# One-hot matrices of the geometric stage: loaded and scaled on ScalarE, or compared and scaled on VectorE

## What is computed

```
# first graph layer (attention)
w = ex / denom[dst]
agg = segment_sum(w[:, :, None] * V[src], dst, num_segments=N)

# second graph layer (geometric)
act = softmax(full)                    # full = 64 scores and 192 zeros
msgs = act * tp2_flat
agg = segment_sum(msgs, dst, num_segments=N)
```

## Time and profile before

| | us |
|---|---|
| median of 3 runs (lowest, highest) | 3384.34 (3380.32, 3385.76) |
| the profiled execution | 3386.62 |
| its span, first to last instruction | 3384.7 |
| PE, DVE, ACT, POOL busy | 2547.7, 2239.3, 1415.8, 1500.8 |

### The profile page before, as it was taken

How to read it: one execution, slowest core, us unless ns; L and a number is a source line. 1 busy time by engine, 2 the same in 40 slices (tenths; PEclk the granted TensorE clock), 3 DMA queues, 4 the chain that set the end, 5 groups by cost and what they waited for, 6 DMA issues and landing times. The chain is left out here.

```text
span 3384.7 us, 46930 instructions
## 1 busy us (share of the span) xinstructions
PE 2547.7 (75%) x13339; PEld 1901.5 (56%) x13339; DVE 2239.3 (66%) x5226; ACT 1415.8 (42%) x5164; POOL 1500.8 (44%) x1409
## 2 busy tenths in 40 slices
PE   6555666634777777775369957999999969999997
PEld 3434454422444444443246845666666658789997
DVE  8655565525888888886866828999999962022221
ACT  1000000000555555556232237888888841233332
POOL 0566666615555545550100025666666503434442
PEclk9965656655788878887679978999999979999999
DMA  4223232276677767773200046666666652322223
GB/s 111 67 53 88 71 88 76 84 40 193 199 211 223 214 199 217 212 214 97 73 0 1 8 142 180 199 199 197 201 200 201 164 159 84 71 46 39 38 36 65
DMA packets 288291, 419.61 MB, mean 124 GB/s; under 512 B 118887, under 2 KB 200651, under 8 KB 287720
## 3 DMA queue, kind: packets, MB, share of 16 engines
q0 software_dynamic: 91456, 234.61, 24.5%
q1 hardware_dynamic: 167218, 180.43, 20.0%
q10 hardware_dynamic: 29366, 1.56, 0.8%
HBM read 358.58 MB, written 61.03 MB: 124 GB/s over the span
## 5 line engine op out<-in xcount | busy, mean ns | idle before, releaser
L1314 POOL DMA_INDIRECT g_rows<-h_d,src x416 | 452.8, 1088 | 550.5 <-POOLq L74 319.0
L966 POOL DMA_INDIRECT a_strip<-kv_d,src x416 | 402.1, 966 | 423.0 <-DVE x L1109 204.9
L326 POOL DMA_INDIRECT rec_d<-o_rec_in,o_place x392 | 398.0, 1015 | 293.6 <-DVE o_place L554 171.6
L997 ACT ACTIVATE x<-a_strip,x 128x64 f32<-128x64 f32 x1664 | 408.4, 334 | 220.5 <-PE a_psv L1042 165.9
L1042 PE MATMUL a_psv<-x 128*125 128x260 f32 x832 | 316.1, 488 | 170.5 <-issue 90.4
L410 PE MATMUL o_ps_base<-o_run,o_lo_hot_t 125*128 125x26 f32 x782 | 172.2, 374 | 211.5 <-issue 109.1
L1042 PEld LDWEIGHTS a_psv<-x 128*125 128x125 f32 x832 | 156.0, 223 | 258.6 <-issue 135.4
L410 PEld LDWEIGHTS o_ps_base<-o_run,o_lo_hot_t 125*128 125x128 f32 x782 | 160.2, 304 | 221.2 <-issue 114.4
L1412 PE MATMUL g_psa<-g_msg,g_hot 128*125 128x256 f32 x832 | 232.4, 403 | 56.6 <-issue 52.2
L1022 PE MATMUL a_psq<-q,a_ht 125*128 x1248 | 221.7, 339 | 21.5 <-DVE a_ht L1100 15.6
L1412 PEld LDWEIGHTS g_psa<-g_msg,g_hot 128*125 128x125 f32 x832 | 140.1, 188 | 172.8 <-issue 159.3
(11 more groups left out here) (436 smaller groups left out, 5441.5 us busy)
## 6 DMA issues: line engine op xcount, KB each, us to landing
a_row<-rows_d SPq DMA_DIRECT2D x104, 256.0 KB
hot_d<-x SPq DMA_DIRECT2D x104, 250.0 KB
g_hot<-hot_d SPq DMA_DIRECT2D x104, 250.0 KB
o_row<-dst_rows_d SPq DMA_DIRECT2D x98, 256.0 KB
o_row_lo<-lo_rows_d SPq DMA_DIRECT2D x98, 128.0 KB
e_w<-in_L_ffn_W1p SPq DMA_DIRECT2D x8, 1024.0 KB
e_w<-in_L_ffn_W2p SPq DMA_DIRECT2D x8, 1024.0 KB
a_strip<-kv_d,src POOLq DMA_INDIRECT x416
```

Of the source, the lines that this page charges most:

```text
L326: pool.indirect_dma_start(out=m.rec_d[:, :], out_offset=bass.IndirectOffsetOnAxis(ap=place[s % RP][:, u:u + 1], axis=0), in_=rec_in[:, U * ...
L966: pool.indirect_dma_start(out=strip[:, lane.start + u, place:place + 2, :].rearrange("p a d -> p (a d)"), out_offset=None, in_=m.kv_d[:, : ...
L997: act.activation(msg[b][:, u, h, 0:HD], strip[:, lane.start + u, place, h * HD:(h + 1) * HD], ACT.Copy, scale=w[:, k * U + u, h:h + 1])
L1314: pool.indirect_dma_start(out=rows[r][:, u, 64:576], out_offset=None, in_=m.h_d[:, :], in_offset=bass.IndirectOffsetOnAxis(ap=m.src[:, s * ...
```

## The change

The attention stage no longer stores `hot`, and the DRAM tensor `hot_d` is gone. The geometric stage no longer loads it. There DVE makes `hot` with four tensor_scalar instructions per step, one per group: the row of node numbers 0 to 124 is compared with the edge's number and multiplied by the reciprocal `rz`, both per-partition numbers. They stand behind the fourth addition and ahead of L1498. ACT's four L1363 are gone, and `s_xm` is raised by the last L1358. PE waits for the new semaphore too.

```diff
@@ attention
-        s_kept = [sem(f"a_kept{b}") for b in range(2)]
...
-        KEEP = LAG + R
...
-            for s in range(STEPS + KEEP):
-                if s < STEPS:
-                    if s >= R:
-                        sp.wait_ge(s_ht, s - R + 1)
-                    sp.dma_start(rowb[s % R][:, :], m.rows_d[s:s + 1, :].to_broadcast([128, 2 * W])
-                                 ).then_inc(s_row[s % R], 16)
-                v = s - KEEP
-                if v >= 0:
-                    sp.wait_ge(s_hot, v + 1)
-                    sp.dma_start(m.hot_d[v], hot[v % 2]).then_inc(s_kept[v % 2], 16)
-            for b in range(2):
-                sp.wait_ge(s_kept[b], 16 * len(range(b, STEPS, 2)))
+            for s in range(STEPS):
+                if s >= R:
+                    sp.wait_ge(s_ht, s - R + 1)
+                sp.dma_start(rowb[s % R][:, :], m.rows_d[s:s + 1, :].to_broadcast([128, 2 * W])
+                             ).then_inc(s_row[s % R], 16)
...
                 if s >= 2:
                     dve.wait_ge(s_mm, U * (s - 1))
-                    dve.wait_ge(s_kept[s % 2], 16 * (s // 2))
@@ geometric
-        s_hot = [sem(f"g_hot_{r}") for r in range(RH)]
+        s_hot = sem("g_hot")
...
-        @block.sync
-        def _(sp):
-            for s in range(STEPS):
-                if s >= RH:
-                    sp.wait_ge(s_prod, 2 * (s - RH) + 2)
-                sp.dma_start(hot[s % RH][:, :, :], m.hot_d[s]).then_inc(s_hot[s % RH], 16)
...
                 for u in range(U):
-                    act.activation(msg[s % RM][:, u, 64:256], vec[b][:, u, :], ACT.Copy, scale=en[s % 3][:, u:u + 1])
-                h = hot[s % RH]
-                act.wait_ge(s_hot[s % RH], 16 * (s // RH) + 16)
-                act.wait_ge(s_rz, 2 * s + 2)
-                for u in range(U):
-                    last = act.activation(h[:, u, :], h[:, u, :], ACT.Copy, scale=rz[b][:, u:u + 1])
+                    last = act.activation(msg[s % RM][:, u, 64:256], vec[b][:, u, :], ACT.Copy, scale=en[s % 3][:, u:u + 1])
                 last.then_inc(s_xm, 1)
...
                     pe.wait_ge(s_xm, s + 1)
+                    pe.wait_ge(s_hot, s + 1)
...
                 add(3)
+                if not last:
+                    if s >= RH:
+                        dve.wait_ge(s_prod, 2 * (s - RH) + 2)
+                    dve.wait_ge(s_rz, 2 * s + 2)
+                    for u in range(U):
+                        t = s * U + u
+                        done = dve.tensor_scalar(hot[s % RH][:, u, :], m.iota[:, 0:P], m.rec[:, t, R_LO:R_LO + 1],
+                                                 rz[b][:, u:u + 1], ALU.is_equal, ALU.mult)
+                    done.then_inc(s_hot, 1)
                 if not last:
                     dve.tensor_tensor(t1[:, :, :], t1[:, :, :], ps_o[b][:, :, 0:64], ALU.add).then_inc(s_t1, 1)
@@ build
-        m.hot_d = dram("hot_d", [STEPS, EP, U, P])
```

## The result

The changed kernel takes **3493.93 us**, the median of 4 runs (3491.08 to 3497.41); the kernel before, on the same chip, 3382.33 (3377.04 to 3385.76). The ratio is 1.0332, 95% interval [1.0313, 1.0351]: slower by 3.3%. The forecast was 3488 within 3436 to 3530.

A forecast was written before the change was run, and what follows sets the result against it. It took DVE's own instruction stream to bound the geometric stage. Added comparisons 110 us, less 5 for attention and 1 at the end, gave +104: 3488 us, measured from the median 3384.34, with a range of 3436 to 3530.

The forecast's parts named there:

- The main term: Geometric stage: four added DVE instructions paid in full, 0.27 us each, 1.08 a step over 102 steps, 110 us.
- The rivals by price: Geometric comparisons: 0.15 us each gives 3439 us, chance 0.10; 0.36 each, the whole duration, gives 3525 us, chance 0.12.
- The new waits cost nothing.: Geometric stage, DVE: waiting for `s_rz` and `s_prod` adds 0 us, the fourth addition covering the reciprocal.
- never waits: Geometric stage: DVE, busy 97% of the steady stretch, waits for no other engine in a step of 6.58 us.
- by the same 1.08 us: Geometric stage: DVE's stream after the comparisons, POOL's gathers and PE all move by 1.08 us a step.
- Attention: Attention stage: removing the stores of `hot` gains 5 us, with bounds of 0 and 95.5 us.
- attention pays it back: Rival: attention regains 95.5 us of DVE's idle time, leaving 3390 us, no measurable change; chance 0.05.
- The start: Start of the geometric stage: DVE idles 13.15 and 0.95 us in the first two steps, so 102 steps pay.
- The 1 us at the end: End of the geometric stage: DVE's wait of 1.31 us for PE before the last additions shrinks, gaining 1 us.
- TensorE's clock: Steady geometric stretch: PE's busy share falls from 92% to 79%, its granted clock staying at 1.00.
- The condition of the rival: Geometric stage: PE's clock falls, costing time below 0.79; at 0.75 it adds 45 us, giving 3533; chance 0.06.
- The other signs: Steady geometric stretch: period 7.6 to 7.7 us, DVE at 97% or more, ACT idling 1.3 us more plus the longer step.

The follow-up runs named there:

- e2: The changed kernel without the four comparisons per step, the one-hot buffers holding ones; 3384.10 us, ratio 1.0010 to the kernel before.
- e5: The changed kernel with the comparisons' factor a constant 0.005 instead of the reciprocal from `rz`, leaving one per-partition number; 3265.52 us, ratio 1.0239 to the kernel before.
- e3: The changed kernel with GpSimd's geometric gathers waiting for the product instead of the second vector addition; 3486.47 us, ratio 1.0315 to the kernel before.
- e1: The changed kernel with attention's stores of `hot` and their waits put back, nothing reading them; 3495.38 us, ratio 1.0339 to the kernel before.
- e9: The changed kernel unaltered, run again on another chip beside the kernel before; 3299.40 us, ratio 1.0355.
- e12: The kernel before with the addition to `t1` moved ahead of the fourth addition, a repeat on another chip; 3157.62 us, ratio 0.9887.
- e4: The changed kernel with the four comparisons moved between the addition to `t1` and the product; 3443.72 us, ratio 1.0197 to the kernel before.
- e8: The kernel before with only the addition to `t1` moved ahead of the fourth addition; 3154.00 us, ratio 0.9893.
- e7: The kernel before with the addition to `t1` ahead of the fourth addition and the next step's maximum ahead of the product; 3158.00 us, ratio 0.9898.
- e10: The changed kernel with one 128x500 comparison, ScalarE's scaling kept, and the addition to `t1` ahead of the fourth addition; 3214.83 us, ratio 1.0081 to the kernel before.

## Why the prediction was right, point by point

**The main term.** "Four tensor_scalar ... on the path in full": shown, by e2 (without them 1.0010) and by the rows (1.02 us between start and start). The price was taken as 0.27, between 0.25 and 0.29; it measured 0.255. Over 102 steps that is 104 us where the sum had 110. The lower of the two rows, the one with no gather beside it, was the right one, although 200 of the 416 comparisons start during a gather: there a gather lengthened the negation, not the comparisons. The rivals by price are out, 0.15 as much as 0.36. The Trainium skill, page "VectorE: DVE Perf Modes", section on the TRN2 errata, would have given the 0.125 us that the prediction quoted as an estimate from it; this case's trace does not agree, with 0.255 for two per-partition operands and 0.195 for one (e5).

**"The new waits cost nothing."** True of the two waits that were added, and yet a wait appeared: this is the term that the sum lacked. The longer step moved the negation into the end of a gather, it took 0.30 instead of 0.17, and ScalarE's chain made L1462 wait that much longer. 0.12 us over the some 90 steps with a gather so placed are 11 us. The prediction could not see this because it held that VectorE "never waits" in this stage; the rows of ScalarE beside those of VectorE show that it waited for this chain already, by 0.09 us a step. The four comparisons pay in full because they stand outside the stretch from the negation to L1462. e3 takes the collision away and gets 0.10 us a step back. The prediction said that POOL's gathers would move "by the same 1.08 us" as everything else; they did not keep their place against the negation.

**Attention.** The term was 5 us with bounds of 0 and 95.5; it measured 0. VectorE's idle time ahead of L1140 and L1100, 95.5 us, is 100.5 in the changed kernel, under the numbers L1130 and L1091:

```profile
L1130 DVE TENSOR_TENSOR agg<-agg,a_psv 125x260 f32 x384 | 160.3, 417 | 56.9 <-DMA lo_rows_d<-o_turned_b 36.0 <-PE a_psv L1033 13.8 <-issue 5.3
...
L1091 DVE TENSOR_SCALAR a_ht<-a_row,part 128x1024 bf16<-128x1024 bf16 x92 | 44.2, 481 | 43.6 <-remote 43.6
```

"DMA lo_rows_d" cannot be what L1130 waits for: that transfer belongs to the sort, and in the program L1130 waits only for TensorE's products, the additions before it and, once in 8 steps, VectorE's own rescaling. The rival "attention pays it back" is out by e1 and e9. Most of the idle time comes neither from the stores nor from the program alone: from 850 to 1390 us the two lines idle for 43.5 and 33.5 us in the changed kernel, and for 17.7 and 0.0 in the same kernel on the chip of e9. In that stretch TensorE stands still for over 2 us at a time 16 times in the kernel before, 13 times in the changed one and 13 times in e1, which has the stores; in e5 to e12 it never does, with the stores or without. What stops it was not found.

**The start.** "In the first two steps DVE idles ... anyway ...; so 102 steps pay." It was the first five: up to the sixth maximum the stage took 65.4 us before and 65.6 after. So 98 distances pay 1.02, 100 us, and with the 11 of the collision 111 us; measured from there to the end are 109.6. The 1 us at the end came as forecast: the wait ahead of the last additions fell from 1.31 to 0.17 us. That 3488 is as near to 3494 as it is, is in part luck. The term of 110 was 10 too large, by the price and by the steps, and the missing collision of 11 made up for it; what is left of the difference is mostly the 5 us that attention did not give back. The mechanism, VectorE's instructions paid in every step with nothing in return, was right.

**TensorE's clock.** The text expected 79% at a granted clock of 1.00. It is 636.80 / 753.67 = 84% at 0.91, between the levels of 1.2 and 2.4 GHz: TensorE's share fell, stretches at the lower clock came in, and its busy time in a step rose with them. The condition of the rival thus came true in part, but not as far as its turning point of 0.79. It cost next to nothing: over the whole stage VectorE's additions L1437 idle for 7.3 us on account of TensorE, and 7.08 of them are one stop at the start, at 2049.79.

**The other signs.** VectorE is busy for 720.97 / 753.67 = 96% of the steady stretch, just under the 97% named, for the wait at L1462. The period is 7.71, just outside of 7.6 to 7.7, for the same reason. ScalarE's idle time went from (643.67 - 569.91) / 98 = 0.75 us a step to (753.67 - 469.25) / 98 = 2.90; "1.3 us more plus the longer step" would be 0.75 + 1.27 + 1.08 = 3.1.

## What to carry to other kernels

When an engine is busy for 97% of a stage, an instruction moved onto it costs its start-to-start time in every step, whatever it relieves elsewhere; take that time from a row of the same form with the same number of per-partition operands. Do not conclude from rows without a named wait that the engine waits for nobody: set the start of each instruction beside the end of what it needs on the other engines. Then look at the short instructions on whose result another engine's chain hangs: a longer step moves them against GpSimd's gathers, and 0.13 us there can come back as a wait. And before adding work to such an engine, look in its order for an instruction that waits for the one just ahead: here two moved lines and a later gather were worth 1.7%.

## What was not expected of the hardware

- **A wait for the direct predecessor costs twice.** A VectorE instruction of 256 columns that waits for the one just ahead starts 0.51 us after it; with another instruction between them, successive ones of this size start 0.33 apart. In addition what stands in the queue behind the waiting one starts later: here a register load of 0.34 us, worth another 0.14 by its times (e4, e8).
- **A gather lengthens a small instruction only at some moments.** The negation (128x4) took 0.17 us outside of gathers and also when it started 0.3 to 0.5 us into one (e4, e5); 0.30 when it started 0.76 in, 0.30 before the end (the changed kernel, e9); 0.40 in e7, 0.5 in and 0.4 before the end; but 0.17 again in e8, 0.7 in and 0.4 before the end. All 252 long ones of the changed kernel, e7 and e9 end together with their gather, to 0.01 us, as if held until then; nearly all the short ones of e4, e5 and e8 that start during a gather end 0.26 to 0.44 us ahead of its end. Why some are held and others not is open. That it takes 0.20 in most steps of e10, where no gather runs, is open too.
- **The same kernel differed by 6% from chip to chip**, 3381 us against 3188 to 3191, in the sort (767 against about 690) and in attention (822 against about 711), not in the dense stage (414 to 416) nor in the geometric period. From 850 to 1390 us, in attention, the mean granted clock of TensorE was 0.81 on the slower chip (the kernel before and the changed one) and 0.90 and 0.89 in e8 and e9, and only on the slower one does TensorE stop as said above. Why was not tried; it does not touch the verdict, since the loss was 111.6 us on the one and 111.9 on the other.
